# Routing the last row too: a fifth group of expert tiles behind the last attention

## The reference

```python
x = x + attention(layernorm(x))              # sin(30 * q.k / sqrt(8)) in place of a softmax, 16 heads
h = layernorm(x)
shared = expert(h, Wg_s, Wu_s, Wd_s)         # silu(h Wg) * (h Wu), times Wd; 128 -> 256 -> 128
probs = sigmoid(h Wr + rb)                   # 8 experts
scores, idx = top_k(probs, 2)                # two experts for each token
out = shared + sum over e of cw[e] * expert(h, Wg[e], Wu[e], Wd[e])
x = x + out                                  # cw[e] is the score where e is one of the two, else 0
```

## Time and profile before

| what | us |
|---|---|
| median of three runs (lowest, highest) | 459.37 (458.67, 459.43) |
| the profiled execution, its time | 458.65 |
| its span from the first to the last instruction | 456.8 |
| TensorE busy in the span | 417.4 (91%) |
| ScalarE | 338.8 (74%) |
| VectorE | 293.5 (64%) |
| GpSimd | 236.8 (52%) |

### The profile page before, as it was taken

The page is one execution under the profiler, slowest core; times in us unless marked ns, Lnnn a source line. Parts: engine busy times, 40 slices in busy tenths (PEclk is TensorE's granted clock), DMA queues, the critical chain, the costliest instruction groups (busy, mean ns, idle before and its releaser), DMA issues.

```text
span 456.8 us, 12304 instructions
## 1 busy us (share of the span) xinstructions
PE 417.4 (91%) x4432; PEld 220.0 (48%) x4432; DVE 293.5 (64%) x999; ACT 338.8 (74%) x470; POOL 236.8 (52%) x308
## 2 busy tenths in 40 slices
PE   2898999999998999999999999999999989999971
PEld 1322223432423345554454455554544588898861
DVE  6878586555636254658666457786475567667894
ACT  1577978978988988688868887778788656765440
POOL 5251542310187333223867585426686778678851
PEclk9999999999999999999999999999999999999995
DMA  6028679926407532684246625992112257651221
GB/s 169 10 86 227 150 223 266 249 82 172 96 30 208 161 64 66 171 202 81 82 130 201 139 66 145 185 197 72 48 47 65 61 114 144 150 141 42 69 61 34
DMA packets 82186, 56.05 MB, mean 123 GB/s; under 512 B 28752, under 2 KB 76496, under 8 KB 82128
## 3 DMA queue, kind: packets, MB, share of 16 engines
q1 hardware_dynamic: 77824, 47.74, 41.1%
q0 software_dynamic: 3584, 7.35, 6.1%
q10 hardware_dynamic: 720, 0.20, 0.2%
HBM read 22.62 MB, written 27.13 MB: 109 GB/s over the span
## 4 chain that ended last, share of the span: by engine, by line
PE 64%; DVE 12%; issue 10%; ACT 9%; POOL 2%; DMA 2%; DVEq 0%; ACTq 0%; SPq 0%; POOLq 0%
PE o_ps L713 20%; PE score L700 11%; ACT attn L975 6%; PE tile_ps L838 4%; PE tile_ps L840 4%; PE tile_ps L839 4%; PE tile_ps L863 3%; DVE hid L1308 2%; DVE x_all L1354 2%; PE r_ps L726 2%; PE r_ps L676 2%; PE r_ps L682 2%; PE r_ps L669 2%; PE tile_ps L865 2%; PE tile_ps L864 2%
## 5 line engine op out<-in xcount | busy, mean ns | idle before, releaser
L975 ACT ACTIVATE attn<-score 128x1024 f32<-128x1024 f32 x256 | 248.2, 1025 | 24.0 <-PE score L700 23.5
L1533 POOL TENSOR_TENSOR hid_lo<-hid,hid_hi 128x256 f16<-128x256 f32 (+1 forms) x94 | 71.8, 764 | 129.0 <-DVE hid_hi L1316 117.3
L713 PE MATMUL o_ps<-attn,vals 128*32 128x512 f32 x1024 | 136.4, 604 | 0.7 <-ACT o_t L982 0.5
L700 PE MATMUL score<-queries,keys 64*128 64x512 f16 x512 | 82.8, 383 | 9.1 <-ACT attn L975 7.6
L1308 DVE SCALAR_TENSOR_TENSOR hid<-tile_ps,gate 128x256 f32<-128x256 f32 (+1 forms) x88 | 40.4, 459 | 48.5 <-ACT gate L996 46.0
L996 ACT ACTIVATE gate<-tile_ps 128x256 f32<-128x256 f32 (+1 forms) x88 | 36.3, 412 | 34.4 <-PE tile_ps L840 33.6
L838 PE MATMUL tile_ps<-xt,w_hi 128*128 128x128 f16 x244 | 43.7, 219 | 0.7 <-ACT y_sb L1008 0.7
L839 PE MATMUL tile_ps<-xt,w_hi 128*128 128x128 f16 x244 | 43.7, 219 | 0.0
L840 PE MATMUL tile_ps<-xt,w_lo 128*128 128x128 f16 x244 | 43.7, 219 | 0.0
L1001 ACT ACTIVATE hid_hi<-hid 128x512 f16<-128x512 f32 (+1 forms) x38 | 23.1, 608 | 27.7 <-DVE hid L1308 26.5
L700 PEld LDWEIGHTS score<-queries,keys 64*128 64x128 f16 x512 | 17.9, 94 | 52.5 <-ACT attn L975 33.4
(11 more groups left out here) (223 smaller groups left out, 963.7 us busy)
## 6 DMA issues: line engine op xcount, KB each, us to landing
q_four<-q_parts SPq DMA_DIRECT2D x14, 256.0 KB
queries<-q_four SPq DMA_DIRECT2D x14, 256.0 KB
k_four<-k_minus SPq DMA_DIRECT2D x14, 256.0 KB
keys<-k_four SPq DMA_DIRECT2D x14, 256.0 KB
y_sorted<-y_sb SPq DMA_DIRECT2D x52, 64.0 KB
x_sorted<-zeros SPq DMA_DIRECT2D x2, 1472.0 KB, 8.5
queries<-q_three SPq DMA_DIRECT2D x14, 192.0 KB
keys<-k_three SPq DMA_DIRECT2D x14, 192.0 KB
```

The costliest lines, as they stand in the source:

```text
L700: mm = pe.matmul(score[h][:, i, :], keys[b % 2][rows, 2 * j + h, kt * P:(kt + 1) * P], queries[b % 2][rows, 2 * j + h, :], start=True, sto ...
L713: mm = pe.matmul(o_ps[32 * i:32 * i + 32, :], vals[b % 2][:, kt, h:h + 32], attn[k % RING][:, i, :], start=(k == 0), stop=(k == UNITS - 1))
L975: act.activation(attn[k % RING][:, 2 * (u % 2):2 * (u % 2) + 2, :], score[u % 2][:, :, :], ACT.Sin, scale=SIN_SCALE).then_inc(sined, 1)
L1533: pool.tensor_tensor(cells(hid_lo, d), cells(hid, d), cells(hid_hi, d), ALU.subtract).then_inc(lo_by_pool, 1)
```

## The change

Row 7 becomes group 4, routed like the others, with 8 scatters, 15 tiles in 8 jobs and 8 gathers. In the new plan the tail has jobs 76 to 105: 76 to 96 as before, 97 to 104 the tiles of group 4, and 105 the second pair of row 7's shared expert. Gate and up of job 97 stands in slot 42, of 104 in 56, of 105 in 58; the last `down` is in slot 66.

The steps of row 7 stand closer and earlier (the E_ constants): logits in slot 15, choose in 17, ranks in 18, parts and places in 19, tile experts in 21, shares in 27. The scatters of group 4 take slots 24, 25, 27, 28, 30, 31, 33 and 34, and its loads stand in slots 37 to 51. Gathers: 11 of group 1 in slots 7 to 22 and one in 36; of group 2 in 37 to 60; of group 3 in 61 to 72; of group 4 in 73 to 84. Combining begins in slot 16 for row (1, 0), 41 for (1, 1), 53 for (2, 0), 65 for (2, 1), 77 for (3, 0) and 88 for (4, 0). Group 3 is no longer the last, and so uses the shared area of y_back. Before the first scatter of group 4 GpSimd also waits for the loads of group 2.

Low halves in the tail, before: on GpSimd for jobs 76, 77, 78, 81, 84, 87 to 92 and every third from 95 on, else on VectorE. After: on GpSimd for 76, 78, 79, 81, 82, 84, 85 and 86, and on VectorE for 77, 80, 83 and all from 87 on.

The diff, cut to its core (a line of dots stands for what is left out; TensorE's loop also calls `ranks` for group 4 in slot E_PREFIX):

```diff
-E_COPYO, E_OUT, E_RES, E_POW2, E_APPLY2, E_XHI, E_XLO = 1, 4, 5, 6, 8, 11, 13
-E_XT2, E_COPYX2, E_ROUTE, E_LOGIT, E_TANH, E_TOP, E_CHOOSE = 16, 17, 20, 21, 21, 23, 25
-E_TILES = 26
+E_COPYO, E_OUT, E_RES, E_POW2, E_APPLY2, E_XHI, E_XLO = 1, 4, 5, 6, 7, 9, 10
+E_XT2, E_COPYX2, E_ROUTE, E_LOGIT, E_TANH, E_TOP, E_CHOOSE = 12, 13, 14, 15, 15, 16, 17
+E_PREFIX, E_DISPATCH, E_SCATTER = 18, 19, 24
...
-ROUTE_GROUPS = [(0, 1), (2, 3), (4, 5), (6,)]
-DENSE = 7
+ROUTE_GROUPS = [(0, 1), (2, 3), (4, 5), (6,), (7,)]
...
+    if ROUTE_GROUPS[g][-1] == ROWS - 1:
+        return TAIL + E_SCATTER + k + k // 2
     return SLOTS * (ROUTE_GROUPS[g][-1] + 1) + S_SCATTER + k + k // 2
...
-        out.append("r" if a >= TAIL + E_CHOOSE + 4 and out[-1] == "o" else "o")
+        out.append("r" if a >= TAIL + E_DISPATCH + 4 and out[-1] == "o" else "o")
...
     if g == len(ROUTE_GROUPS) - 1:
-        return last + 6
-
-    return max(last + 8, TAIL + 16) if last + 8 >= TAIL else last + 8
+        return last + 4
+
+    return max(last + 5, TAIL + 16) if last + 8 >= TAIL else last + 8
...
-LO_DVE = [d for d in HI_ACT if GU_SLOT[d] + 2 in _gathering or GATHER_SLOT[-1][-1] <= GU_SLOT[d] <= GATHER_SLOT[-1][-1] + 3]
+_moving = _gathering | {scatter_slot(g, k) for g in range(len(ROUTE_GROUPS)) for k in range(SCATTERS[g])}
+LO_DVE = [d for d in HI_ACT if GU_SLOT[d] + 2 in _moving and GU_SLOT[d] + 3 in _moving or GU_SLOT[d] >= TAIL + E_SCATTER and (GU_SLOT[d] + 2 in _moving or GU_SLOT[d] + 3 in _moving)]
...
-                for t in range(0, TT, 2):
-                    if D_SLOT[JOBS.index((FULL, DENSE, t, ROUTED - 1, 2))] == a:
-                        store_last(t)
...
-                    pe.wait_ge(logit_ready, ROWS)
+                    pe.wait_ge(pos_ready, len(ROUTE_GROUPS))
...
-                dve.wait_ge(weight_ready, ROWS)
-                wait_read(dve, JOBS.index((FULL, row, t, e - 1, 2) if e else (SHARED, row, t, None, 2)))
-                for m in range(2):
-                    ins = dve.scalar_tensor_tensor(out=x_tile(row, t + m), in0=here[:, m * DM:(m + 1) * DM], scalar=weight[len(ROUTE_GROUPS) % 2][:, t + m, e:e + 1],
-                                                   in1=x_tile(row, t + m), op0=ALU.mult, op1=ALU.add)
-                ins.then_inc(d_read, 1)
...
+                if tail == E_DISPATCH:
+                    parts(len(ROUTE_GROUPS) - 1)
+                    places(len(ROUTE_GROUPS) - 1)
+                if tail == E_DISPATCH + 2:
+                    tile_experts(len(ROUTE_GROUPS) - 1)
+                if tail == E_DISPATCH + 8:
+                    shares(len(ROUTE_GROUPS) - 1)
...
+                    if g == len(ROUTE_GROUPS) - 1:
+                        for n, (group, _, _) in enumerate(LOADS):
+                            if group == g - 2:
+                                pool.wait_ge(xt_loaded[n % XT], 16 * (n // XT + 1))
```

More of the change, by code:

```diff
@@ L111, in scatter_slot @@
 def scatter_slot(g, k):
+    if ROUTE_GROUPS[g][-1] == ROWS - 1:
+        return TAIL + E_SCATTER + k + k // 2
     return SLOTS * (ROUTE_GROUPS[g][-1] + 1) + S_SCATTER + k + k // 2
 SCATTERS = [2 * TT * len(rows) for rows in ROUTE_GROUPS]
-SHARED, SPARSE, FULL = "shared", "sparse", "full"
+SHARED, SPARSE = "shared", "sparse"
 def plan():
-    shared = [(SLOTS * (j + 1) + S_COPYX2 + 3, (SHARED, j, t, None, 1)) for j in range(ROWS - 1) for t in range(TT)]
-    sparse = [(scatter_slot(g, SCATTERS[g]) + 8, (SPARSE, g, i, None, 1)) for g in range(len(ROUTE_GROUPS)) for i in range(GTILES[g])]
+    shared = [(SLOTS * (j + 1) + (S_COPYX2 if j < ROWS - 1 else E_COPYX2) + 3, (SHARED, j, t, None, 1)) for j in range(ROWS) for t in range(TT)]
+    sparse = [(scatter_slot(g, SCATTERS[g]) + (8 if g < len(ROUTE_GROUPS) - 1 else 6), (SPARSE, g, i, None, 1)) for g in range(len(ROUTE_GROUPS)) for i in range(GTILES[g])]
     jobs, slots = [], []
@@ L139, in in_twos @@
         return out
-    sparse, late = in_twos(sparse), [job for _, job in in_twos(shared)]
-    dense = [(SHARED, DENSE, t, None, 2) for t in range(0, TT, 2)] + [(FULL, DENSE, t, e, 2) for t in range(0, TT, 2) for e in range(ROUTED)]
+    sparse, late = in_twos(sparse), in_twos(shared)
     a = TAIL
-    while sparse or late or dense:
+    while sparse or late:
         if sparse and sparse[0][0] <= a:
             jobs.append(sparse.pop(0)[1])
[L147 to L150, removed]
+        elif late and late[0][0] <= a:
+            jobs.append(late.pop(0)[1])
         else:
@@ L786, in piece @@
                     return part[:, :, :].rearrange("p e n -> p (e n)")[:, bass.ds(place_of[row, t + m], P)]
-                return part[:, own(e + 1 if kind == FULL else 0), :]
+                return part[:, own(0), :]
             placed = set()
@@ L948, in _ @@
                     route(ROWS - 1)
+                if tail == E_PREFIX:
+                    ranks(len(ROUTE_GROUPS) - 1)
         @block.scalar
@@ L1236, in choose @@
                 dve.wait_ge(top_step, step + 4)
[L1237 to L1238 removed]
+                dve.tensor_scalar(mask[g % 2][:, t0:t0 + TT, :], rest[:, :, 0:ROUTED], -1.5, None, ALU.is_lt).then_inc(mask_ready, 1)
                 dve.scalar_tensor_tensor(out=weight[g % 2][:, t0:t0 + TT, :], in0=rest[:, :, 0:ROUTED], scalar=-1.5,
@@ L1332, in read_down @@
                 mine = x_all[:, (row * TT + t) * DM:(row * TT + t + n) * DM]
[L1333 to L1336, removed]
-                dve.wait_ge(weight_ready, ROWS)
-                wait_read(dve, JOBS.index((FULL, row, t, e - 1, 2) if e else (SHARED, row, t, None, 2)))
-                for m in range(2):
-                    ins = dve.scalar_tensor_tensor(out=x_tile(row, t + m), in0=here[:, m * DM:(m + 1) * DM], scalar=weight[len(ROUTE_GROUPS) % 2][:, t + m, e:e + 1],
-                                                   in1=x_tile(row, t + m), op0=ALU.mult, op1=ALU.add)
-                ins.then_inc(d_read, 1)
+                dve.wait_ge(x1_done, row + 1)
+                dve.scalar_tensor_tensor(out=mine, in0=here, scalar=DOWN_UNSCALE, in1=mine, op0=ALU.mult, op1=ALU.add).then_inc(d_read, 1)
             def combine(g, row, t, c):
```

9 lines of the change are left out of this document (3 added, 6 removed).

## The result

The changed kernel takes **468.61 us** (median of 4 runs, 466.76 to 468.73) against 459.36 us (4 runs of the kernel before beside it, 458.67 to 459.43). The ratio is 1.019, with a 95% interval of 1.0174 to 1.0207: slower by 9 us. The prediction was 463.7 us, with a range up to 467.5. The direction was right, but the size was 4.9 us short, and the measured time lies 1.1 us past the end of the range. The profiled execution took 468.73 us around a span of 466.9, so 1.83 us lies outside the span, as in the kernel before.

The account below looks back on a forecast made before the run. TensorE bounds the kernel before; afterwards GpSimd's queue with its waits: group 2 done 428.4, 2.9 waiting, 16 gathers (20.0) to 451.3, 9.8 to a 461.1 span, plus 1.85 and 0.7: 463.7 us, range 457.5 to 467.5.

Parts of the forecast that it names:

- The floor: GpSimd's queue in the tail, nothing stopping it: last gather done at 446.5, plus 9.8 us, a span of 456.3.
- three waits across the queues: Tail: SyncE's y store waits on slot 36, group 4's loads go out late, GpSimd's gathers wait for VectorE's combining.
- (a): Group 3's first y store waits for group 1's last gather in slot 36, landed 407.5; job 91's copy at 409.2.
- (c): Group 3's first gather, slot 61, waits 2.9 us for row (2, 0)'s combining, at 431.3; shared y_back rows.
- 373.70 + 21.2 = 394.9: GpSimd before the scatters: 11 gathers, 5 pair low halves and a single, 21.2 us from 373.70.
- the part on VectorE: VectorE, slots 15 to 21: 11.3 us of work in 7 to 8; job 86's hidden tile 391.7, places 390.8.
- about 1 us more: Price of VectorE's low halves meeting GpSimd's gathers on the shared port; left out of the sum, kept in the range.
- about 1.0 us after its instruction: When a GpSimd gather's data is there, read from the DMA slices: 437.23 to 438.18 shows up to 439.3.
- the seven jobs: From job 97's hidden tile at 415.1 to job 104's: seven at 2.04 us, 14.3, plus 1.0 combining, giving 430.4.
- Rival 3: Queues stall further, by the shared port or a later scatter block delaying slot 36: 465 to 468 us; chance 0.15.
- Rival 1: The cross-queue waits do not bite and GpSimd runs through: 458.9 us, no difference; chance 0.26.
- Rival 2: TensorE still sets the end and GpSimd's queue hides: 452.4 us; chance 0.12 with a smaller mechanism at 457.5.

Follow-up runs that it names:

- both: Changed kernel with a third y_sorted buffer and an own place for group 3's gathers: 460.97 us, ratio 1.0053 to the kernel before.
- lo79_b: Repeat on another chip of the changed kernel with only job 79's low half moved to VectorE: 467.70 us, ratio 1.0186 to the kernel before.
- early_e: Kernel before, row 7 still dense, with row 7's transposition and routing steps in the change's earlier slots: 460.74 us, ratio 1.0025 to the kernel before.
- old_lo: Changed kernel with low halves of jobs 79, 82, 85, 86 back on VectorE and 77 on GpSimd: 462.32 us, ratio 1.0081 to the kernel before.
- third_y: Changed kernel with a third y_sorted buffer: 464.46 us, ratio 1.0136 to the kernel before.
- no_g4: Changed kernel without group 4's eight gathers, so row 7 gets wrong expert sums: 462.13 us, ratio 1.0074 to the kernel before.
- lo79: Changed kernel with only job 79's low half moved to VectorE, on a slower chip: 500.41 us, ratio 1.0429 to the kernel before.
- after_b: Changed kernel itself, unedited, run again on another chip: 470.13 us, ratio 1.0227 to the kernel before.
- sc25: Changed kernel with scatters starting at slot 25 instead of 24, group 1's last gather back in slot 23: 463.33 us, ratio 1.009 to the kernel before.
- own_back: Changed kernel with group 3's gathers in a place of their own, the free attn buffer: 463.54 us, ratio 1.0116 to the kernel before.
- both_old_lo: Changed kernel with third y_sorted buffer, own place for group 3's gathers, low halves of jobs 76 to 86 as before: 457.61 us, ratio 0.996.
- sc25_own_lo_b: Changed kernel, scatters from slot 25, group 3's own place, low halves of 79, 80, 82, 83, 85, 86 and from 87 on VectorE: 455.90 us.
- sc25_own_lo: First run, on a slower chip, of the kernel of sc25_own_lo_b: 505.57 us, ratio 1.0513 to the kernel before.

## Why the prediction was right or wrong

**The mechanism was right in the main.** GpSimd's queue sets the end. The floor forecast from it, 456.3, is 457.9 in `both`, but that they lie so close is luck: there the last gather ends at 451.0, forecast 446.5, and from it to the end it is 6.9, forecast 9.8, two misses that nearly cancel. The three waits across the queues are all there, SyncE's for slot 36, ScalarE's copy behind it, and GpSimd's for row (2, 0), and taking away (a) or (c) gave back 5.1 and 6.4 us of span. That (a) would strike a second time, at group 4's own y stores, was missed: they were to be stored by 437 and landed by 445.86. TensorE is done at 443.8 (forecast 437), the gathers are 1.25 apart (the whole of group 4 in the rows below, which answer), and the chain of waits ends in them.

```profile
L1548 POOL DMA_INDIRECT y_back<-y_sorted,place4a x4 | 3.9, 968 | 1.2 <-issue 1.2
```

**The sizes were wrong**, and they add up. In the order of the sum:

- Slot 36's gather ends at 409.81, forecast 406.5: **+3.3**. The step that failed is "373.70 + 21.2 = 394.9": the 11 gathers and the low halves between them were added up back to back, with nothing for the time in which GpSimd waits for a high half. They run from 374.15 to 398.04, where the scatters begin, so 0.45 is a later start and 2.7 mostly the waiting (three waits of 0.46, 1.35 and 1.92, less the gaps that they replace). Behind it is the part on VectorE, which had the hidden tile of job 86 at 391.7 and the places at 390.8; they come at 394.99 and 394.16. VectorE is held up by GpSimd's low halves for some 4.0 us (above) and delivers its hidden tiles late, ScalarE then its high halves. `lo79_b` shows the first of these 1.5 us at slot 36: with it gone, less the 0.6 of the low half that VectorE now does itself, the gather there ends 1.1 earlier. The rest of the scatters' block was sized well (11.8 from 398.04 with the gather of slot 36, forecast 11.6). The port was left out of the sum as "about 1 us more", for gathers on GpSimd's side only.
- The copy of job 91 comes at 414.86, forecast 409.2: another **+2.4**. I read "about 1.0 us after its instruction" off the DMA slices, and the 1.65 of the store off; there the data stops moving. The semaphore comes later: the gather that ends at 409.81 lets the store go at 412.23, so 2.4, and the store issued there lets ScalarE go after 2.6, where I had 1.65.
- Hidden tiles of job 96 and 97 come at 417.30 and 421.16, forecast 411.6 and 415.1: +5.7 and +6.1. The load took 4.51 from issue to landing (413.82 to 418.32 in the chain of waits; 3.88 in the earlier trace rows), and TensorE's clock fell (below). Job 104 stands at 437.16, forecast 430.4, and row (2, 0) is combined at 437.83, forecast 431.3: **+6.5**. So the seven jobs were sized well, 16.0 us in all against 15.3, with part of the lower clock in it.
- From there to the end of the last gather 22.1, forecast 20.0: **+2.1**. It is mostly the gap of 1.84 us, where 0.30 is usual (+1.5), and 0.8 from VectorE's last operation to the first gather.
- From there to the span's end 6.93, forecast 9.8: **-2.9**. The last operations of the changed kernel, and SyncE's waits at the end, first before and then after:

```profile
461.51 0.35 DVE L1339 SCALAR_TENSOR_TENSOR x_all<-y_back,share4a,x_all 128x128 f32<-128x128 f32 x1 [7.34 <-DMA y_back<-y_sorted,place4b]
...
463.85 0.35 DVE L1339 SCALAR_TENSOR_TENSOR x_all<-y_back,share4b,x_all 128x128 f32<-128x128 f32 x1
464.23 0.37 SPq L601 DMA_DIRECT2D out<-x_all  x1
```

```profile
SPq L328 <- PEq L328: 3.8, 1, 3.8
SPq L328 <- DMA out<-x_all: 1.2, 1, 1.2
```

```profile
SPq L327 <- DMA out<-x_all: 1.7, 1, 1.7
...
SPq L327 <- PEq L327: 0.2, 1, 0.2
```

 The landing took 1.54 (461.51 less 459.97), the combining 2.7, and from the store at 464.23 the end comes 2.7 later. I had taken 4.2 us behind the last store's data from the earlier trace rows as a price of ending. It was a wait on TensorE's sequencer: 3.8 us in the two kernels with a dense row 7 (the one before and `early_e`), where TensorE's last matmul ends close to VectorE's last operation (450.28 and 450.93 in the kernel before), and 0.2 in all routed ones, where TensorE is done long before (443.8 in the changed kernel). Whether the early end or something else in the routed program takes it away was not tried apart. SyncE's waits of before would have shown it.

Together +3.3 +2.4 +0.8 (from +5.7 to +6.5) +2.1 -2.9 = +5.7, the 5.8 us between the spans. The median of the runs is 0.1 below the profiled execution's time, where I had added 0.7, and so the miss is 4.9.

**The rivals.** Rival 3 (465 to 468) came nearest, 0.6 us short of the 468.61 measured. Its reason, that each us late at slot 36 counts in full, is what `old_lo` bears out (5.3 there, 6.8 of span). Rival 1, that the waits don't bite, fell; its time is that of `both`, where they are taken away (span 457.9, forecast 456.3). Rival 2 fell: the spacing of 1.24 to 1.25 holds in the best version too. The range bore either of the two misses (463.7 + 3.3 = 467.0, 463.7 + 2.4 = 466.1), but not both at once, though the rows for both were there: a short landing was read from slices only.

## What to carry to other kernels

When a change moves work to another engine, write out that engine's whole queue to the last instruction before counting the gain: here some 17 us of TensorE's work became 20 of GpSimd's, 16 indirect DMAs at 1.25 to 1.29. Then go through the shared buffers that the moved work pushes into other queues, since a single late gather held up SyncE, ScalarE, TensorE and at last GpSimd itself, one behind another. Where two engines can hold each other up, count it from both sides. Read a landing from what the waiting engine does next, not from the moment at which the data stops; and ask of every constant at the end of a span which semaphore it is.

## What the runs showed of the chip

- **A GpSimd tensor operation stops VectorE.** Four 128x128 f32 operations took 2.80 us beside a low half of 1.17 and 1.27 without it; a combining operation took 2.01 instead of 0.35, and a scan of three small ones (128x8) 1.42 instead of 0.57. Two of them had started before the low half, by 0.76 and 0.69 us, and ended 0.09 and 0.16 behind it.
- **The clock falls behind a short idle time.** TensorE was busy 0.94 and 0.46 of 2 us in 414 to 416 and 416 to 418, waiting 1.06 us for ScalarE's copy (until 415.62) and 2.14 for the loads (until 418.60). The granted clock then fell, after it had taken up work again:

```profile
416.00:418.00 2.00, 0.46 (x9) 0.28 (x6) 1.46 (x5) 1.26 (x4) 1.39 (x3) 1.00 1.21 146
418.00:420.00 2.00, 1.40 (x22) 1.41 (x23) 1.47 (x4) 0.63 (x1) 1.70 (x2) 0.89 0.79 195
420.00:422.00 2.00, 2.00 (x21) 2.00 (x20) 0.84 (x2) 0.98 (x3) 0.32 (x1) 0.50 0.62 175
422.00:424.00 2.00, 2.00 (x30) 2.00 (x29) 1.59 (x5) 1.07 (x2) 0.00 (x0) 0.76 0.51 132
```

 In 420 to 422 it was 0.50, that is 1.2 of 2.4 GHz. Matmuls stand 0.11 us apart there and 0.055 at 419; from 419.6 to 422.9 half of 3.3 us is lost, some 1.6.
- **Landings.** A gather's semaphore comes 2.8 us after its start (434.50 to 437.28 in the chain of waits), and 2.5 in the quiet end. By the Trainium skill, "DMA: Bandwidth & Descriptors", section "Anatomy of one DMA — SWDGE (gpsimd) path", such a DMA takes about 2.0 us and its bytes at 436 GB/s, which for 64 KB would be an estimated 2.15; measured it is 0.3 to 1.2 more (408.83 to 412.2 with the DMA engines busy).
- **1.8 us behind the first gather of group 3** (1.84; the same in `third_y`, `old_lo`, `no_g4`, `lo79`, `lo79_b` and `after_b`, 1.77 in `sc25`) stand in every kernel in which group 3 gathers into y_back rows that group 2 had. They are not there in `own_back`, `both`, `both_old_lo` and `sc25_own_lo_b`, where it has its own place, but `sc25_own_lo`, the same kernel on the slower chip, has its own place and 1.86 us. So the shared rows can't be the whole reason, and what it is stays open.
